# Order and unused places of the expert blocks, and the queue that stores their results

## The reference, cut to what matters

```
logits = xf @ Wg + bg
topv, topi = jax.lax.top_k(logits, K)            # K = 2, E = 8
wts = jax.nn.softmax(topv, axis=-1)
order = jnp.argsort(-wts[:, 0])
cap = int(CAP_RATIO * T / E)                     # 15680
keep = pos < cap                                 # pos: place in the list of the expert
h = gelu(einsum('ecd,edf->ecf', eb, W1) + b1)    # 128 -> 512
y = einsum('ecf,efd->ecd', h, W2) + b2           # 512 -> 128
```

## Time and profile before

| | us |
|---|---|
| median of 3 runs | 7258.95 (7255.88 to 7261.76) |
| the profiled execution | 7259.78 |
| its span in the trace | 7257.9 |
| PE busy | 5066.4 (70%) |
| DVE busy | 2421.7 (33%) |
| ACT busy | 1540.1 (21%) |
| POOL busy | 1893.5 (26%) |

### The profile page before, as it was taken

One profiled execution on the slowest core, in us unless ns is written; L12 is line 12 of the kernel. 1 busy time (PEld: TensorE's weight loads), 2 busy tenths in 40 slices (PEclk: granted clock), 3 DMA queues, 4 the chain that ended last, 5 costly groups with the idle time before them and its releaser, 6 DMA issues. The chain is left out here.

```text
span 7257.9 us, 77541 instructions
## 1 busy us (share of the span) xinstructions
PE 5066.4 (70%) x20517; PEld 2657.6 (37%) x20517; DVE 2421.7 (33%) x4879; ACT 1540.1 (21%) x3769; POOL 1893.5 (26%) x1983
## 2 busy tenths in 40 slices
PE   9999991200100008888888777777776999999999
PEld 3655591100000004333333333333343555454454
DVE  0022269910000002111221112111127667777664
ACT  2233364200000002222222222222220111111111
POOL 0000002277777770000000000000005444444441
PEclk9999995555555559898999999999997999999999
DMA  8877792143333331111111111111115444444441
GB/s 172 183 191 193 178 262 88 59 139 116 122 119 116 118 111 52 50 50 50 50 50 50 50 50 50 50 50 50 50 53 190 144 147 154 148 145 151 151 140 55
DMA packets 1026572, 788.13 MB, mean 109 GB/s; under 512 B 592849, under 2 KB 934786, under 8 KB 1022082
## 3 DMA queue, kind: packets, MB, share of 16 engines
q1 hardware_dynamic: 874546, 421.96, 21.8%
q0 software_dynamic: 84224, 257.01, 10.9%
q10 hardware_dynamic: 67408, 105.16, 4.2%
HBM read 444.05 MB, written 339.75 MB: 108 GB/s over the span
## 5 line engine op out<-in xcount | busy, mean ns | idle before, releaser
L1413 PE MATMUL cp<-padded,taps_o 128*128 128x448 f32 x4032 | 1578.3, 547 | 62.5 <-DVE padded L1601 62.5
L1109 PE MATMUL xt_ps<-ident_e,rows_in 128*128 128x128 f32 x1040 | 182.4, 300 | 1676.3 <-DMA rows_in<-xy 1675.8
L1167 ACT ACTIVATE hid<-hid_ps,b_cols 128x512 f32<-128x512 f32 (+1 forms) x1056 | 717.2, 681 | 2748.5 <-PE hid_ps L1117 2747.0
L1125 PE MATMUL y_ps<-hid,w_sb 128*128 128x512 f32 (+1 forms) x2112 | 1078.6, 660 | 0.4 <-DVE yt L1192 0.4
L1413 PEld LDWEIGHTS cp<-padded,taps_o 128*128 128x128 f32 x4032 | 758.0, 191 | 783.6 <-issue 749.5
L1186 DVE COPY xt<-xt_ps 128x512 f32<-128x512 f32 (+1 forms) x264 | 180.4, 684 | 2516.9 <-PE xt_ps L1109 2516.9
L1117 PE MATMUL hid_ps<-xt,w_sb 128*128 128x512 f32 (+1 forms) x2112 | 939.2, 587 | 3.0 <-DVE xt L1186 3.0
L1380 POOL DMA_INDIRECT y_ring<-xy,index_o x784 | 799.2, 1019 | 244.2 <-issue 241.1
L448 POOL DMA_INDIRECT xy<-twice,slots x784 | 770.0, 982 | 255.9 <-issue 255.1
L1109 PEld LDWEIGHTS xt_ps<-ident_e,rows_in 128*128 128x128 f32 x1040 | 117.0, 148 | 1887.2 <-DMA rows_in<-xy 1453.9
L80 POOL MEMSET ident_o<- 128x128 f32 x1 | 0.2, 207 | 2731.9 <-POOLq L992 2731.9
(11 more groups left out here) (311 smaller groups left out, 3598.5 us busy)
## 6 DMA issues: line engine op xcount, KB each, us to landing
rows_in<-xy SPq DMA_DIRECT2D x1040, 64.0 KB, 1.8
xy<-rows_out SPq DMA_DIRECT2D x1040, 64.0 KB, 1.6
xin<-in_x_dram SPq DMA_DIRECT2D x256, 196.0 KB
conv<-rows ACTq DMA_DIRECT2D x256, 196.0 KB
pix<-conv SPq DMA_DIRECT2D x224, 224.0 KB, 5.1
xn<-hat SPq DMA_DIRECT2D x112, 448.0 KB, 4.5
chunk<-xn POOLq DMA_DIRECT2D x112, 448.0 KB, 3.7
logits<-xn SPq DMA_DIRECT2D x112, 448.0 KB, 4.2
```

The costliest lines, as they stand in the source:

```text
L1109: last = pe.transpose(xt_ps[e % 2][:, k * 128:(k + 1) * 128], rows_in[e][:, k, :], ident[:])
L1125: last = pe.matmul(y_ps[:, 0:cols], w2_sb[e][:, f, :], hid[e % 2][:, f, 0:cols], start=(f == 0), stop=(f == NH - 1))
L1167: act.activation(hid[e % 2][:, f, 0:cols], hid_ps[f][:, 0:cols], ACT.Gelu, bias=b1_cols[:, e * NH + f:e * NH + f + 1]).then_inc(hid_ready, 1)
L1413: last = pe.matmul(cp[i % 2][:, 0:HB * W], taps[:, t, :], padded[b][:, img, hb * HB + kh:hb * HB + kh + HB, kw:kw + W], start=(t == 0), st ...
```

## The change

**The order of the blocks.** Before, the blocks of an expert are ordered by (k+1) divided by the rows of their class, for block k, a ratio that is worked out with reciprocals and compared over all pairs of classes; the unused places stand behind the last block. Now DVE notes, at each of 28 marks of four chunks, how many blocks of each class are complete. A running sum over marks and classes gives each block its rank in the order of completion, and the place of rank 0 is moved so far back that the last block stands at place 129: an expert with fewer than 130 blocks has its unused places first. The number of chunks that a block needs is rounded up to a multiple of four; an unused place needs one. ACT's count of chunks and its copies into `pay`, the 64 comparisons `spots` on DVE, and the small matmuls on PE that summed the table (L750, L752) are gone; a seventh PSUM bank is free for `class_ranks`.

**The stores.** They move from SP to ACT, which issues those of tile t-3 (`BACK`) behind its four gelus of tile t. The four addresses of a tile are now read by one register load of four registers (`addresses`), on both engines.

```diff
+POSITIONS_USED = 130
...
-            act.wait_ge(limit_set, 1)
-            for c in range(CLASSES):
-                last = act.activation(sign_out[:, c, :], run[:, c, 1:GR], ACT.Sign, bias=limit_c[:, c:c + 1], scale=-1.0,
-                                      accum_out=parts[:, 2, c:c + 1])
...
+            do(dve.tensor_scalar(marks[:, :, 1:MARKS], run[:, 0:CLASSES, STEP:GR:STEP], 1.0 / 128, -0.5 + 1.0 / 256, ALU.mult, ALU.add))
+            whole_part(marks[:, :, 1:MARKS])
+            do(dve.tensor_tensor(marks[:, :, MARKS], block_at, blocks_c[:], ALU.add))
...
-            for e in range(E):
-                for o in range(E):
-                    last = dve.tensor_scalar(spots[:, e * E + o, :], ramp[:], pos[:, e, o:o + 1], None, ALU.is_equal)
-                last.then_inc(spots_set, 1)
...
+            do(dve.tensor_tensor(fresh, seen[:, :, E:], seen[:, :, 0:EDGE], ALU.subtract))
+            do(dve.tensor_tensor_scan(flat(done_by), flat(edge_on[:]), flat(fresh), 0.0, ALU.mult, ALU.add))
+            do(dve.tensor_tensor(shift, seen[:, :, E:], done_by, ALU.subtract))
...
+            do(dve.tensor_tensor(flat(fresh)[:, 0:last_i], flat(shift)[:, 1:], flat(shift)[:, 0:last_i], ALU.subtract))
+            for h in range(2):
+                do(dve.tensor_scalar(rank[:, h, :], done_by[:, :, EDGE - 1], rank_base[:, h:h + 1], None, ALU.add))
+            for h in range(2):
+                for e in range(E):
+                    at = rank[:, h, e:e + 1]
+                    dve.scalar_tensor_tensor((shift, sieve)[h][:, e, :], done_by[:, e, :], at, fresh[:, e, :], ALU.is_le, ALU.mult,
+                                             accum_out=moved[:, h, e:e + 1])
+                    last = dve.tensor_scalar(sieve_n[:, h * E + e, :], done_by[:, e, E - 1::E], at, 0.0, ALU.is_le, ALU.add,
+                                             accum_out=passed[:, h, e:e + 1])
...
+            do(dve.tensor_scalar(chunks_f[:], passed[:], float(STEP), float(STEP - 1), ALU.mult, ALU.add))
...
+        def addresses(eng, q, e, way, blocks):
+
+            regs = [eng.alloc_register(f"row{next(numbers)}") for k in range(blocks)]
+            eng.reg_load(regs, tables.where[0:1, bass.ds(q * BLOCKS, blocks), way, e])
+            return [eng.snap(r, donate=True, min_val=0, max_val=2 * ROWS - 256 + 1) for r in regs]
...
-                at = [sp.value_load(tables.where[0:1, bass.ds(q * BLOCKS + k, 1), 0, e:e + 1].rearrange("p q e -> p (q e)"),
-                                    min_val=0, max_val=2 * ROWS - 256 + 1) for k in range(blocks)]
+                at = addresses(sp, q, e, 0, blocks)
...
-                store(t, e, q, LAST if last else BLOCKS)
...
+                if not (first and e < BACK):
+                    store(t - BACK, (e - BACK) % E, q - (1 if e < BACK else 0), LAST if last and e >= BACK else BLOCKS)
+
+            def store(t, e, q, blocks):
+                at = addresses(act, q, e, 1, blocks)
+                act.wait_ge(out_ready, t + 1)
+                for k in range(blocks):
+                    act.dma_start(halves[bass.ds(at[k], 256), :].rearrange("(p h) c -> p h c", h=2)[:, 0, :], rows_out[e][:, k, :]
+                                  ).then_inc(tile_out[e], 16)
```

More of the change, by code:

```diff
@@ L1 @@
 from contextlib import ExitStack
+from itertools import count
 import concourse.bass as bass
@@ L531, in route_phase @@
         zeros = sb("zeros", [128, 2 * C])
[L532 to L535, removed]
+        rows_i = sb("rows_i", [128, 1], I32)
+        blocks_c, tail_block, some, vacant = (
+            sb(n, [128, CLASSES]) for n in ("blocks_c", "tail_block", "some", "vacant"))
@@ L549, in route_phase @@
-        chunks_row = spent[:, 3 * E ** 3:3 * E ** 3 + POSITIONS * E].rearrange("p (q e) -> p q e", e=E)
-        sign_out = both[:, 0:CLASSES * (GR - 1)].rearrange("p (c g) -> p c g", c=CLASSES)
+        edge_on = sb("edge_on", [128, E, EDGE], BF16)
+        rows_c = sb("rows_c", [128, ALL])
+        spent = both.bitcast(F32)
+        fresh, done_by, shift = (spent[:, i * E * EDGE:(i + 1) * E * EDGE].rearrange("p (e i) -> p e i", e=E) for i in range(3))
+        free = area[:, ALL * J // 2:]
+        seen = free[:, 0:E * (EDGE + E)].rearrange("p (e i) -> p e i", e=E)
@@ L951, in _ @@
-            do(dve.scalar_tensor_tensor(pos[:], neg_pos[:], -1.0, missing[:], ALU.mult, ALU.add))
-            for e in range(E):
-                for o in range(E):
-                    last = dve.tensor_scalar(spots[:, e * E + o, :], ramp[:], pos[:, e, o:o + 1], None, ALU.is_equal)
-                last.then_inc(spots_set, 1)
-            dve.wait_ge(table_summed, 1)
-            do(dve.tensor_copy(address[:], tab[:, :, 0]))
-            do(dve.tensor_tensor(address[:], address[:], tab[:, :, 1], ALU.add))
@@ L970, in _ @@
+            dve.tensor_tensor(where_rows[:, :, 1, :], address[:], used[:], ALU.add).then_inc(table_set, 1)
             for i, (c0, c1) in enumerate(RANK_GROUPS):
@@ L1065, in load @@
                                  ).then_inc(tile_in[i], 16)
-            def store(t, e, q, blocks):
-                i = e % RING
-                sp.wait_ge(out_ready, t + 1)
-                for k in range(blocks):
-                    at = sp.value_load(tables.where[0:1, bass.ds(q * BLOCKS + k, 1), 1, e:e + 1].rearrange("p q e -> p (q e)"),
-                                       min_val=0, max_val=2 * ROWS - 256 + 1)
-                    sp.dma_start(halves[bass.ds(at, 256), :].rearrange("(p h) c -> p h c", h=2)[:, 0, :], rows_out[i][:, k, :]
-                                 ).then_inc(tile_out[i], 16)
             for e in range(AHEAD):
```

129 lines of the change are left out of this document (42 added, 87 removed).

## The result

The changed kernel takes **5383.7 us** (median of 4 runs, 5383.1 to 5386.0). Beside it the kernel before took 7258.2, so the ratio is **0.742, 95% interval 0.7405 to 0.7431**; forecast were 5380. The profiled execution has a span of 5381.4 us.

A forecast was written before the change was run, and what follows sets the result against it. Bounds: the chunk count up to 2722, then SP's issuing. Gains 1159.5 + 709 + 13 = 1881.5 us off 7259.8 give 5378, from the median 5377; plus 3 for first loads, 5380 us. Forecast range 5350 to 5430; wider range 5350 to 5520.

The forecast's parts named there:

- Two bounds, one behind the other: Expert phase: up to 2722 the count of scattered chunks binds, from then on SP at 10.53 us from store to store.
- The gain at the start, 1159.5: Start of expert phase: the new block order removes the chunk wait, `up` of tile 4 at 1569.7 instead of 2729.2.
- the route phase: Before the expert phase: DVE's new table work, at most 34 us against 31.3, is hidden by 16.8 us of cover; price 0.
- The period, 709: Steady expert phase: with stores off SP, PE sets the period, 7.75 us a tile instead of 10.56, gaining 709 us.
- the last round: Tiles 256 to 263, half the columns: 31 us on PE alone instead of 44.1, a gain of 13 us.
- ACT's price, 0: ACT in the expert phase: taking over the stores costs nothing; without cover from late gelus, 25 us.
- the lower end of its turn: ACT's turn of gelus and store taken at 5.6 us, not 7.5, assuming a four-register load costs as one.
- The collision: Rival, chance 0.04: tiles and scatter slow each other in the expert phase, the period doubles until the scatter ends; 5953 us.
- My evidence against it, four tiles in 28.5 us: Tiles beside the scatter before: POOL made 0.81 operations per us there against 0.77, taken as no slowing.
- The 6100 for the order alone: Whole kernel with only the start gain and the period left at 10.56; also the rival that moving stores gives nothing, chance 0.03.
- The rule on issuing engines: Skill's rule for the stores' move: several issuing engines save only sequencer time, usually little; it gives a rival's 6100, chance 0.03.
- the 3 us added for the first loads: Start of the expert phase: 3 us added to the sum for the first loads running beside the weights.

## Why the prediction was right, point by point

**Two bounds, one behind the other.** This held. With either part undone the old bound came back: 739.8 us of wait for POOL with the old order, 10.57 us a tile with the stores and the old register loads on SP.

**The gain at the start, 1159.5.** Measured 2729.17 less 1573.22, 1156.0. The count of chunks was right in each of three places where it was tried: the changed order, unused places last, and the old order with unused places first (395 us against some 400). It needs both halves of the edit: completion order alone gives nothing, since tile 4 still has to wait; unused places first alone give two thirds. The 3.5 us that are missing are a later start: `b_cols` is shifted at 1541.28 and not at 1537.45. POOL's eight early chunks ended at 1498.3 and not at 1493.3, and the loss is all in the first, as the start of POOL's second copy shows, before and in the change:

```profile
1411.80 1.69 POOL L442 COPY twice<-chunk 128x1792 f32<-128x1792 f32 x1
1417.23 1.70 POOL L444 COPY twice<-chunk 128x1792 f32<-128x1792 f32 x1
```

The prediction put the route phase at nothing because DVE's new work is covered. That held: DVE is done at 1477.3, where it was at 1476.5. What it did not ask is what this work does to POOL, which opens the phase. From 1406.24 to 1416.39 DVE runs its four new operations over 1792 elements, and four of POOL's indirect DMAs that begin in that stretch take 1.8 to 3.6 us instead of about 1. The eleven kernels and runs with the new table took 18.8 to 19.1 us for the first chunk, the three with the old one 13.2 to 13.4. Which of DVE's operations does it was not tried.

**The period, 709.** Measured 703.7: from `up` of 4 at 1573.22 to `up` of 256 at 3531.57 it is 1958.4 us, against 2662.1 before. All of it runs at 7.75 us a tile but for the one wait of 3.50 us and the slow product behind it. The stores alone measured 725 with the last round, against 722. This step's reason, that SP's own pieces add up to the period, is what the two intermediate kernels bear out: either of the two cures alone, the new form of the register loads or the second queue, brings the steady run behind the scatter to PE's pace.

**ACT's price, 0.** Right, with the lower end of its turn. From the first gelu at 2998.44 to the end of the stores at 3004.06 it is 5.6 us. The pieces are others than the prediction's, so the agreement to a tenth is partly luck: the gelus take 3.3 us and not 2.7, since 0.17 us stand between them, and the stores with what goes before them 2.35 and not 2.9. The reason given for the lower end, that the rows price a load by instruction, could not be read from them, since they hold only loads of one register. The 0.64 us of the prediction is such a load with its arithmetic; the load itself is recorded with 0.27 us in the kernel before as well, less than half of the 600 ns that the prediction found it to agree with. One of four registers is longer, 0.89 us, and begins while ACT's last gelu runs.

**The collision.** The rival had too narrow a form. PE's and POOL's operations do not slow each other: PE is fully busy beside the scatter and POOL's copy takes 1709 ns on average, against 1712 before. What is slower is issuing, 12.8 us a tile instead of 10.6 with the old SP code. My evidence against it, four tiles in 28.5 us, could not show it, for there I looked at POOL's operations alone. The forecast stood because in the change SP and ACT have more slack than the stretching takes; the prediction had not reckoned with it. This is also why the parts do not add up: 936 and 725 alone make 1661, together they give 1874. The 6100 for the order alone was some 220 us too low for the same reason.

**The rule on issuing engines.** "DMA: Bandwidth & Descriptors" in the Trainium skill, section "Issuing engines are not separate DMA queues", would have given 6100 by its "usually small". The change's 5384 does not follow that, since a queue's issuing and register loading were the whole period here. Its other half fits: what the second queue saved is the time of the one that issues, and with the shorter register loads already on SP it was worth only 153 us. The prediction had chosen the rows.

**The last round and the small terms.** 29.4 us from `up` of 256 (3531.57) to `up` of 263 (3560.98), forecast 31, so 14.7 us gained and not 13. Behind DVE's last copy into `rows_out` the kernel took 1814.8 us before and 1812.7 in the change. (The windows say 1808.9 and 1813.4, but begin 5.9 us behind that copy before, and 0.7 us ahead of it here.) The four measured parts, 1156.0 + 703.7 + 14.7 + 2.1, make 1876.5, all of the difference between the two spans. Against the forecast's 1881.5 the start and the period gave 8.8 us less and the two small terms 3.8 more; the 3 us added for the first loads took up more than half of the rest. So the total agrees to 4 us partly by offset.

**Open.** What stretches SP's issuing beside the scatter. The DMA share is 0.49 to 0.59 there, so the engines that move data have room. SP has no more steps to do, and the median one is no longer than before, but some take up to 0.75 us. So with the register loads of its stores in the kernel with the order alone, from 1600 to 2600 and from 2800 to 3300:

```profile
L1032 SPq TENSOR_LOAD <-where x307: 1/270/750, 1602.6 to 2599.7; - x154
L1032 SPq TENSOR_LOAD <-where x188: 263/268/283, 2805.3 to 3297.2; - x188
```

ACT's queue is not spared: in the change the issue of one store takes up to 2.05 us beside the scatter and at most 0.38 behind it. Whether POOL's issuing or the memory traffic does it was not tried apart.

## What to carry to other kernels

Where a scatter or any producer fills a table, count for every consumer how many of the producer's steps it needs, in the order in which they will run, and look for the first one whose number is out of line; one early place that needs the last number, here the first real blocks of a small expert, stops everything behind it. When an engine that only issues transfers has a period of its own, add up its pieces: it can be relieved by fewer or plainer register loads or by a second queue, and the slack that either gives matters more while a scatter runs beside it. Store behind a distance at which the result is already there, since an in-order queue passes each wait on to the computing that stands behind it, and the lower clock makes it dearer.

## What the hardware showed unexpectedly

- A load of four registers from SBUF took 0.87 us on SP's queue and 0.89 on ACT's, a load of one 0.27. ACT's queue began it while the last gelu still ran, so only 0.49 us stood between that gelu and the first store.
- SP's four stores with four register loads took 3.87 us alone and up to 6.92 us beside POOL's scatter, with the median register load unchanged (268 and 270 ns) and the longest 283 and 750 ns.
- POOL's first chunk of the scatter took 18.8 us beside four large operations of DVE, single indirect DMAs up to 3.6 us, where it took 13.2 beside smaller ones.
- With one wait of 3.9 us in each 13.6 us the granted clock was 0.87 to 0.88, and the product behind each wait took 5.40 us instead of 3.60.
